# Mamba scan kernel: the last row summed by transposes as well, one more input product on GpSimd, one small mask moved

## Time and profile before

| | |
|---|---|
| runs | 870.86, 872.44, 872.67 us; median 872.44 us |
| the profiled execution's own time | 870.91 us |
| its span, first to last instruction | 869.2 us |
| mean granted TensorE clock | 0.995 of 2.4 GHz |
| PE, DVE, ACT, POOL busy | 836.9, 690.4, 557.8, 642.8 us |
| the chain that ended last, by engine | PE 36% of the span, all others 1% or less |

### The profile page before, as it was taken

How to read it: one execution, slowest core, us unless ns; L and a number is a source line. 1 busy time by engine, 2 the same in 40 slices (tenths; PEclk the granted TensorE clock), 3 DMA queues, 4 the chain that set the end, 5 groups by cost and what they waited for, 6 DMA issues and landing times. The chain is left out here.

```text
span 869.2 us, 12767 instructions
## 1 busy us (share of the span) xinstructions
PE 836.9 (96%) x3899; PEld 639.7 (74%) x3899; DVE 690.4 (79%) x1271; ACT 557.8 (64%) x1049; POOL 642.8 (74%) x476
## 2 busy tenths in 40 slices
PE   8999999999999999889999997999999999999997
PEld 7678778887877786566566665687887887788885
DVE  6969778776976578999999999887876977776664
ACT  6565565565566658878889893466575556555553
POOL 6958675776675767799998997856767677676755
PEclk9999999999999999999999998999999999999999
DMA  8733474454434252565465553435366435536440
GB/s 215 217 127 110 146 194 117 133 128 140 123 112 134 84 143 95 189 200 184 156 203 192 171 176 140 150 97 170 97 189 185 122 124 155 154 100 190 135 122 25
DMA packets 126421, 126.88 MB, mean 146 GB/s; under 512 B 59400, under 2 KB 83088, under 8 KB 126352
## 3 DMA queue, kind: packets, MB, share of 16 engines
q1 hardware_dynamic: 103648, 120.81, 45.7%
q10 hardware_dynamic: 22704, 5.25, 2.8%
HBM read 116.59 MB, written 9.44 MB: 145 GB/s over the span
## 5 line engine op out<-in xcount | busy, mean ns | idle before, releaser
L810 POOL TENSOR_TENSOR act_lo<-act,act_hi 128x512 fp32r<-128x512 f32 x288 | 372.1, 1297 | 188.8 <-ACT act_hi L921 186.9
L914 ACT ACTIVATE bank<-bank 128x512 f32<-128x512 f32 x252 | 146.7, 582 | 234.9 <-PE bank L1249 226.7
L1145 DVE TENSOR_TENSOR sg<-bank,c_ring 128x512 f32<-128x512 f32 x252 | 172.5, 684 | 97.7 <-ACT bank L914 95.3
L1245 PE MATMUL bank<-x_parts,w_hi 128*128 128x512 f32 x572 | 231.7, 405 | 3.3 <-DVE sg L1145 2.1
L1123 DVE SCALAR_TENSOR_TENSOR act<-sg,bank 128x512 f32<-128x512 f32 x288 | 197.8, 687 | 41.7 <-PE bank L1249 20.7
L1249 PE MATMUL bank<-x_parts,w_hi 128*128 128x512 f32 x572 | 226.1, 395 | 0.0
L1246 PE MATMUL bank<-x_parts,w_lo 128*128 128x512 f32 x572 | 226.1, 395 | 0.0
L921 ACT ACTIVATE act_hi<-act 128x512 fp32r<-128x512 f32 x286 | 178.1, 623 | 0.4 <-PE bank L1221 0.4
L1245 PEld LDWEIGHTS bank<-x_parts,w_hi 128*128 128x128 f32 x572 | 107.4, 188 | 36.5 <-DVE sg L1145 4.7
L1249 PEld LDWEIGHTS bank<-x_parts,w_hi 128*128 128x128 f32 x572 | 107.5, 188 | 26.0
L1246 PEld LDWEIGHTS bank<-x_parts,w_lo 128*128 128x128 f32 x572 | 107.5, 188 | 25.6 <-issue 1.7
(11 more groups left out here) (186 smaller groups left out, 996.6 us busy)
## 6 DMA issues: line engine op xcount, KB each, us to landing
c_ring<-c_dram SPq DMA_DIRECT2D x252, 256.0 KB, 3.6
c_ring<-c_dram SPq DMA_DIRECT2D x64, 512.0 KB, 4.5
b_slots<-c_dram SPq DMA_DIRECT2D x8, 512.0 KB, 3.8
y_dram<-out_t SPq DMA_DIRECT2D x56, 64.0 KB, 2.8
y_tok<-y_dram SPq DMA_DIRECT2D x14, 256.0 KB, 3.7
xt_dram<-xn ACTq DMA_DIRECT2D x40, 64.0 KB, 3.5
xt<-xt_dram ACTq DMA_DIRECT2D x10, 256.0 KB, 2.8
out<-x_sb SPq DMA_DIRECT2D x7, 256.0 KB, 2.5
```

Of the source, the lines that this page charges most:

```text
L810: self.nc.gpsimd.tensor_tensor(m["act_lo"][:, g % LAG], m["act"][:, g % ACTS], m["act_hi"][:, g % LAG].bitcast(FP32), ALU.subtract).then_i ...
L914: nc.scalar.activation(self.h_bank[:, g % 2], self.h_bank[:, g % 2], ACT.Silu).then_inc(self.sg_ready, 1)
L1145: nc.vector.tensor_tensor(m["sg"][:, g % 2], silu, weight, ALU.mult).then_inc(self.w_done, 1)
L1245: nc.tensor.matmul(dst, m["w_hi"][:, k, n, :], x_hi, start=True, stop=False)
```

## The change

- **Row 7 is summed by transposes like the others.** `TURNED` and `ADDED` go. The pairs of row 7 get 8 transposing pieces each, GpSimd's two additions (L1523) go, and the D·u term uses 4 pieces. The sum of row 7 is turned back in f2's first blocks: DVE copies the transposed sum to SBUF (`dve_turned_y`, after f2 block 2), PE turns it back (after its block 3), DVE copies it again (`dve_back_y`, after block 3). `PE_TAIL` is 1, 2, 3, 4 (sum 62, sum 63, turn back, project) and `DVE_TAIL` 2, 3, 4.
- **Row 0's moved pair uses slot 1**, so that slot 0 is first used by row 1, and the slot load for row 1 waits for no scan.
- **The mask of f2's first row, rank < 2, is made by GpSimd** as a sixth step of `pool_groups`.
- **Row 7 has two moved pairs**: pair 2 in slot 0 (loaded and multiplied where pair 4's was before) and pair 4 in slot 1 (loaded by SP at n == 7 of row 6, multiplied by GpSimd at n == 1 of row 7, `MULT_STEP`).

```diff
-TURNED = 0, 1, 2, 3, 4, 5, 6
-ADDED = ((),) * 7 + ((PAIRS - 2, PAIRS - 1),)
-MOVED = ((6,),) + ((4,),) * 7
+MOVED = ((None, 6),) + ((4,),) * 5 + ((4,), (2, 4))
+MULT_STEP = 1
...
-                    if g in (2, 4):
+                    if g in DVE_TAIL:
                         next(tail)
...
-                    if g in (2, 3, 4):
+                    if g in PE_TAIL:
                         next(tail)
...
+PE_TAIL = 1, 2, 3, 4
+DVE_TAIL = 2, 3, 4
...
-    POOL_STEPS, MORE_STEPS = 5, 2
+    POOL_STEPS, MORE_STEPS = 6, 2
...
         s.do(nc.gpsimd.tensor_tensor(by_group(g_rank), halves[:, :, :, 0], halves[:, :, :, 1], ALU.add))
+        s.settle()
+        s.do(nc.gpsimd.tensor_scalar(m["g_in"][:, 0:TT * GROUPS], g_rank, float(TOP_GROUPS), None, ALU.is_lt))
...
-        s.settle()
-        s.do(nc.vector.tensor_scalar(g_in.rearrange("p (t g) -> p t g", t=nt), g_rank, float(TOP_GROUPS), None, ALU.is_lt))
-        if not by_pool:
+            s.settle()
+            s.do(nc.vector.tensor_scalar(g_in.rearrange("p (t g) -> p t g", t=nt), g_rank, float(TOP_GROUPS), None, ALU.is_lt))
             yield
...
+    def uses_slot(self, i, n):
+        return n < len(MOVED[i]) and MOVED[i][n] is not None
...
                         if i == 0:
-                            self.load_slot(sp, 0, 0)
+                            self.load_slot(sp, 0, 1)
...
                 if i == 0 and n == 4:
-                    self.pool_input(pool, 0, 0)
-                if n == 1:
+                    self.pool_input(pool, 0, 1)
+                if i and n == MULT_STEP:
                     self.pool_input(pool, i, 1)
...
-                product = nc.gpsimd.tensor_tensor(state, state, m["c_ring"][:, 2 * (n % RING):2 * (n % RING) + 2], ALU.mult)
-                if n in ADDED[i]:
-                    product.then_inc(self.weighted, 1)
-                    pool.wait_ge(self.weighted, sum(map(len, ADDED[:i])) + ADDED[i].index(n) + 1)
-                    nc.gpsimd.tensor_tensor(state[:, 0], state[:, 0], state[:, 1], ALU.add).then_inc(self.mul_done, 1)
-                else:
-                    product.then_inc(self.mul_done, 1)
+                nc.gpsimd.tensor_tensor(state, state, m["c_ring"][:, 2 * (n % RING):2 * (n % RING) + 2], ALU.mult
+                                        ).then_inc(self.mul_done, 1)
...
-    def dve_skip_term(self, dve, i):
-
+    def dve_turned_y(self, dve, i):
         dve.wait_ge(self.sum_done, (i + 1) * PAIRS)
-        need(dve, self.out_ready, i)
-        self.nc.vector.tensor_copy(self.m["y_sb"][:, :], self.y_acc).then_inc(self.y_ready, 1)
+        dve.wait_ge(self.turned_back, i)
+        self.nc.vector.tensor_copy(self.yt_sb.rearrange("p t d -> p (t d)"), self.y_acc).then_inc(self.yt_ready, 1)
+
+    def dve_back_y(self, dve, i):
+        dve.wait_ge(self.turned_back, i + 1)
+        dve.wait_ge(self.out_ready, i)
+        self.nc.vector.tensor_copy(self.m["y_sb"][:, :], self.misc).then_inc(self.y_ready, 1)
...
     def dve_tail(self, dve):
-        self.dve_skip_term(dve, BATCH - 1)
+        self.dve_turned_y(dve, BATCH - 1)
+        yield
+        self.dve_back_y(dve, BATCH - 1)
         yield
...
         pe.wait_ge(self.x_added, BATCH - 1)
+        self.pe_turn_back(pe, BATCH - 1)
+        yield
         self.pe_project_out(pe, BATCH - 1, range(TT))
         yield
```

More of the change, by code:

```diff
@@ L1415, in slot_uses @@
     def slot_uses(self, i, n):
-        return sum(len(pairs) > n for pairs in MOVED[:i])
+        return sum(self.uses_slot(j, n) for j in range(i))
+    def uses_slot(self, i, n):
+        return n < len(MOVED[i]) and MOVED[i][n] is not None
     def inputs_before(self, g):
@@ L1425, in load_slot @@
     def load_slot(self, sp, i, n):
-        if n >= len(MOVED[i]):
+        if not self.uses_slot(i, n):
             return
-        earlier = [j for j in range(i) if len(MOVED[j]) > n]
+        earlier = [j for j in range(i) if self.uses_slot(j, n)]
         if earlier:
@@ L1583, in act_soft, with act_turned_y @@
                                   ).then_inc(self.delta_ready, 1)
-    def act_y(self, ae, i):
+    def act_turned_y(self, ae, i):
         ae.wait_ge(self.sum_done, (i + 1) * PAIRS)
-        need(ae, self.out_ready, i)
-        self.nc.scalar.activation(self.m["y_sb"][:, :], self.y_acc, ACT.Copy).then_inc(self.y_ready, 1)
-    def act_turned_y(self, ae, i):
-        n = TURNED.index(i)
-        ae.wait_ge(self.sum_done, (i + 1) * PAIRS)
-        need(ae, self.turned_back, n)
+        need(ae, self.turned_back, i)
         self.nc.scalar.activation(self.yt_sb.rearrange("p t d -> p (t d)"), self.y_acc, ACT.Copy
@@ L1680, in act_pairs @@
                     self.act_decays(ae, g + 2)
-                if n == 4 and i - 1 in TURNED:
+                if n == 4 and i:
                     self.act_back_y(ae, i - 1)
@@ L1849, in pe_add_states @@
             pe.wait_ge(self.setup.diag_done, 1)
-        u, last_n = self.m["u"][:, i % 3], PAIRS - 1
+        u = self.m["u"][:, i % 3]
         if n == 0:
-            if i - 1 in TURNED:
-                pe.wait_ge(self.yt_ready, TURNED.index(i - 1) + 1)
-            else:
-                need(pe, self.y_ready, i)
-            if i in TURNED:
-                for t in range(TT):
-                    cols = slice(t * P, (t + 1) * P)
-                    self.nc.tensor.matmul(self.y_acc[:, cols], u[:, cols], self.m["d_diag"][:, :], start=t == 0, stop=False,
-                                          skip_group_check=True)
-            else:
-                self.nc.tensor.matmul(self.y_acc, self.m["d_diag"][:, :], u, start=True, stop=False, skip_group_check=True)
@@ L1863, in pe_add_states @@
-        pe.wait_ge(self.mul_done, g + 1)
-        if i in TURNED:
-            for s in range(2):
-                for t in range(TT):
-                    cols = slice(t * P, (t + 1) * P)
-                    last = self.nc.tensor.matmul(self.y_acc[:, cols], self.state(g)[:, s, cols], self.m["ident"][:, :],
-                                                 start=False, stop=n == last_n and s == 1, is_transpose=True,
-                                                 skip_group_check=True)
-            last.then_inc(self.sum_done, 1)
-            return
@@ L1873, in pe_add_states @@
-        for s in range(1 if n in ADDED[i] else 2):
-            last = self.nc.tensor.matmul(self.y_acc, self.m["ident"][:, :], self.state(g)[:, s, :], start=False,
-                                         stop=(n == PAIRS - 1 and s == (0 if n in ADDED[i] else 1)), skip_group_check=True)
+            need(pe, self.yt_ready, i)
+            for t in range(TT):
+                cols = slice(t * P, (t + 1) * P)
+                self.nc.tensor.matmul(self.y_acc[:, cols], u[:, cols], self.m["d_diag"][:, :], start=t == 0, stop=False,
+                                      skip_group_check=True)
@@ L1876, in pe_add_states @@
+        pe.wait_ge(self.mul_done, g + 1)
+        for s in range(2):
+            for t in range(TT):
+                cols = slice(t * P, (t + 1) * P)
+                last = self.nc.tensor.matmul(self.y_acc[:, cols], self.state(g)[:, s, cols], self.m["ident"][:, :],
+                                             start=False, stop=n == PAIRS - 1 and s == 1, is_transpose=True,
+                                             skip_group_check=True)
         last.then_inc(self.sum_done, 1)
     def pe_turn_back(self, pe, i):
-        pe.wait_ge(self.yt_ready, TURNED.index(i) + 1)
+        pe.wait_ge(self.yt_ready, i + 1)
@@ L1987, in pe_pairs @@
                         self.pe_conv(pe, i + 1, 1, [2, 3], self.z_bank(i + 1))
-                if n == 3 and i - 1 in TURNED:
+                if n == 3 and i:
                     need(pe, self.xt_copied, min(i + 3, BATCH))
```

5 lines of the change are left out of this document (2 added, 3 removed).

## The result

| | before | after |
|---|---|---|
| runs beside each other | 869.83 to 872.67, median 871.65 us | 866.01 to 867.12, median 866.37 us |
| ratio, 95% interval | | 0.9945 [0.9927, 0.9963] |
| the profiled execution, its span | 870.91, 869.2 us | 866.32, 864.6 us |
| mean granted clock | 0.995 | 0.995 |

The change makes the kernel faster by 0.55%. The forecast was 868.1 on a median of before of 872.44, a gain of 4.3 us. The medians of the runs beside each other differ by 5.28 us, with an interval of the ratio that allows 3.2 to 6.4; the profiled executions differ by 4.59. Of the 1.7 us by which the time came out under the forecast, 0.8 is the median of before, which is 871.65 with one run more; the rest is gain beyond the 4.3.

The account below looks back on a forecast made before the run. DVE was taken to bound the scan stage and PE the feed-forward stage behind it. Terms -1.76 - 2.0 - 1.12 + 0.5 = -4.4 us, taken as -4.3, brought the median of 872.44 to 868.1 us; range 865.6 to 871.0.

Parts of the forecast that it names:

- Part 1: Row 0 in slot 1: no slot load delays C, so row 1's scans 11 to 13 look like row 6's, -1.76 us.
- Part 2: Mask on GpSimd before the product of pair 56: DVE is no longer held by that product, -2.0 us.
- Part 3: Pair 2 of row 7 moved: DVE loses one input product, -1.12 us; GpSimd's lag is felt by PE, not DVE.
- Part 4: Row 7 summed by transposes: pairs 56 to 61 save PE 0.85 us each; without this PE would be late.
- PE and DVE now meet: At the last scan, 552.6 us: PE's sum 62 ends just then; no wait taken, 0.5 us as its bound.
- Part 5: Behind the last scan: +0.2 to block 3, -0.66 for sum 63, +0.95 for the turn back, together +0.5 us.
- slack of 0.5 us: At row 7's projection: DVE's second copy ends at 560.3 us, PE comes behind block 4 at 560.8.
- (a): Row 1's wait comes from PE's queue order at row 0's turn back, not C: part 1 gives nothing, 869.9 us; chance 0.11.
- (b): A slow-clock stretch of 3 us on PE's path behind 543.1 us costs +1.9, giving 870.0 us; chance 0.10.
- (c): PE's clock stays at 1.2 GHz between 543.1 and 558.5 us: costs 9.7 us, time 877.8 us; chance 0.06.
- (d): Behind the last scan, GpSimd holds DVE's two copies, 2.12 us each: gain only 1.1, time 871.3 us; chance 0.11.
- (e): More gain: PE gains its 0.5 us in full and the mask is cheaper, 867.5 us; chance 0.04.

Follow-up runs that it names:

- u_row0: The changed kernel with row 0's moved pair back in slot 0, so SP's slot load for row 1 waits for a scan again: 867.6 us, 0.9961 of before.
- mask_poolwaits: The changed kernel with the mask back on DVE and GpSimd waiting for it before the product of pair 56: 866.27 us, 0.9946 of before.
- act_back: The changed kernel with the second copy of row 7's y made by ACT instead of DVE: 866.14 us, 0.9942 of before.
- both: The changed kernel with the changes of act_back and mask_poolwaits together: 866.04 us, 0.9944 of before.
- both_row2: The kernel both with a second moved pair in row 2 (pairs 2 and 4): 864.34 us, 0.9925 of before.
- u_pair2: The changed kernel with only pair 4 of row 7 moved, pair 2 not: 867.95 us, 0.996 of before.

## Why the prediction was right, and where not

**Part 1, row 0's slot (-1.76 predicted, -1.39 measured).** The mechanism was right: u_row0 brings the C wait and DVE's wait back together. The size was not. The step that failed is "row 1 looks like row 6", by which both waits of row 1 were put down to C, and the term was 7.44 less 5.68. Only the 1.28 before pair 12 hangs on it. The 0.46 before pair 13 is in every kernel, with the lag and without: from pair 11 to 13 pass 6.05 us after the change. I had taken row 6 as the likeness of row 1 because rows 2 to 6 are alike; what is different in row 1 was never shown. ACT's, PE's and GpSimd's rows around that scan stand at the same distance from the scan before in row 2, where there is no wait. Its cause is open.

**Part 2, the mask (-2.0, measured -2.01).** Right, in size and mechanism. mask_poolwaits shows the mechanism by itself: 0.17 against 2.31 us for the same instruction, by nothing but the order. The 0.26 us of GpSimd's step was near the 0.21 of its neighbour.

**Part 3, pair 2 of row 7 (-1.12, measured -1.14).** Right, and so is the sentence that DVE would not feel GpSimd's lag but PE would: PE waits 0.5 to 0.8 us before sums 57, 59, 62 and 63. What the prediction didn't ask is how far this goes: in row 5 the same step was lost again, in row 2 it was kept.

**Part 4, the transposes (no amount of their own, but without them PE would be late).** Right in direction. Taken out they cost 0.70 us, and made alone they bring nothing. "PE and DVE now meet" was half a microsecond off to the good side: PE waited 0.84 us before sum 62, so PE was early, and the 0.1 us that was taken off the gain for the meeting was not needed.

**Part 5, behind the last scan (+0.5, measured +0.04).** The terms of PE's own work were 1.03 us too dear, and a wait of 0.58 us for the second copy, which had been put at nothing, gave more than half of it back. Predicted were +0.2 to block 3, -0.66 for sum 63 and +0.95 for the turn back. Measured, in the same order of places:

- last scan to block 3: 5.36 before, 5.68 after, +0.32.
- block 3 to block 4: 561.08 - 558.82 = 2.26 before, 555.96 - 554.12 = 1.84 after, -0.42 where +0.29 was predicted. The turn back took 0.56 us, not 0.95: its four loads, 0.59 us, were released at once, since the copy was there, and the rows taken for it had an idle time of 0.29 that belonged to their place, not to the operation. And block 3 itself became 0.32 shorter (1.60 to 1.28). I hadn't counted this at all. It is the second load of the block that shows it, 0.43 us behind the first before and 0.11 after; the weight loads of before (with the first load of its projection), then of after:

```profile
559.25 0.19 PEld L1246 LDWEIGHTS bank<-x_parts,w_lo 128*128 128x128 f32 x1 [0.24 <-issue]
...
563.38 0.42 PEld L1890 LDWEIGHTS bank<-w_out_sb,y_sb 128*128 128x128 f32 x2
```
```profile
554.23 0.19 PEld L1248 LDWEIGHTS bank<-x_parts,w_lo 128*128 128x128 f32 x1
```

- block 4 to block 5: 4.20 before, 4.34 after. Here lies the wait for the second copy, 0.58 us more between two loads than without it, against the same 0.32 at the block's first loads and 0.12 at the projection's.

The slack of 0.5 us that the prediction gave the second copy wasn't there, but not because the copy was late. "By the same steps behind block 3" held: the copy was to end 4.35 us behind the start of block 3 (560.3 against 552.65 + 3.3), and it ended 4.34 behind it (558.46 - 554.12), ACT's silu and DVE's wait of 1.26 us for it included; the first copy has 4.40 behind block 2. What failed is PE's side. From block 3 to the projection PE was to take 4.85 us (560.8), and without the wait it would have taken 3.82: the turn back was 0.39 shorter than forecast, and blocks 3 and 4 were 0.32 shorter each (block 4: 2.30 before, 1.98 after). PE came 1.03 us early for a copy with a slack of 0.5. act_back, which ends the copy 1.04 us sooner, takes the wait away and gives 0.44 us behind the last scan.

**Rivals.** (a) fell with u_row0. (b), a slow stretch on PE's path: there is one of about 7 us, but it lies before 540 us; both against both_row2 shows it to cost at most 0.04. In u_pair2 the clock is 0.87 between 540 and 550 us, so slow work reaches further, and there too the way from the last scan to block 5 has the same 11.86 us. (c), a clock that stays down under transposes: it is 1.00 in every stretch looked at from 540 to 850 us. The Trainium skill, TensorE: Matmul & The Clock Gate, section "Part 4: PE-mode transpose", has it that a transpose does not count as busy in the same way; nothing here bears that out, as sums 59 to 63 by transposes ran at 2.4 GHz amid f2's matmuls; a stretch of transposes alone, which would test it, is in no run. (d), copies that are held by GpSimd: both read PSUM and took 0.68, though GpSimd's L813 was running beside each. (e): the meeting of PE and DVE cost nothing, but the mask wasn't cheaper than the forecast had it; that the median lies under the 867.5 of this rival is in part before's median, as said above.

**The sum.** -1.76 - 2.0 - 1.12 + 0.5 = -4.4 was predicted from the first scan on, and measured -4.49: part 1 was 0.37 too large and the tail 0.46 too dear. That these two nearly cancel is luck; the parts 2 and 3 were right by themselves. The first scan was 0.49 us earlier, by stage 1's own scatter, and some 0.4 were given back in f2, so the span became 4.6 shorter.

## What to carry to other kernels

A small instruction that is long in one place and short in all others is to be looked at beside what the neighbour engine does at that moment: 2.31 us here, cured by order alone. Moving work from a full engine to one with 10% to spare paid in row 2 and not in row 5; ask for the busy time by stretch of the receiver in the next stretch as well, and for the small steps in its queue for which a third engine waits. Taking work from an engine that waits brought nothing until the engine it waits for had become faster, so measure such a part with the others in place and also alone. And a slack between two engines is the difference of two chains: here the copy came when it was forecast, and the wait arose because the chain of the engine that wants it had been taken 1.03 us too long. Terms taken too dear are not on the safe side there.

## What was unexpected of the hardware

- A GpSimd product of 128x1024 held a DVE tensor_scalar of 16 columns from SBUF to SBUF for its whole length (2.31 against 0.17 us), when it had started first, even by 0.07 us. DVE instructions with an input in PSUM beside such products were not held (L1033, 0.23 us).
- The first two weight loads of an fp32r block of f2 are 0.43 us apart behind a sum whose moving operand is 512 columns of fp32 with the identity as weights, and 0.11 apart behind one by transposes. This is worth 0.32 us at each change of form.
- Stretches at 1.2 GHz behind waits of PE came and went between kernels whose work in that stretch is alike (0.66 in `both`, 1.00 in `both_row2`, between 530 and 540 us).
